# Projections, running sums and output projection as four column strips of 32 on TensorE

## The reference, cut to what matters

```python
# 8 batches, 512 tokens, 256 features, 16 heads of 16; everything f32
qkv = x @ w_qkv.T                      # q, k, v
L   = (q @ k^T) / 4                    # per head
L_y = (q @ (x @ w_ky.T)^T) / 4
agg = sum(exp(clip(L_y, -15, 15)) * mask) + 1e-6
w   = softplus(log(|L| + 1e-6) - log(agg + 1e-6)) * mask
A   = w / (sum(w) + 1e-6)
x   = layernorm(x + (A @ v) @ w_proj.T)
h   = silu(lin1(x)) * lin2(x)          # 256 -> 1024
h   = gelu(lin_h1(h)); h = gelu(lin_h2(h))
x   = layernorm(x + lin3(h))           # 1024 -> 256
```

## Time and profile before

| | |
|---|---|
| median of 3 runs | 1381.5 us (1379.47 to 1383.17) |
| profiled execution | 1381.93 us, its span 1380.1 us |
| PE busy | 1271.8 us (92%), 8310 matmul records |
| DVE busy | 720.5 us (52%) |
| ACT busy | 616.0 us (45%) |
| POOL busy | 118.2 us (9%) |
| mean granted TensorE clock | 0.985 |

### The profile page before, as it was taken

The page is one execution under the profiler, slowest core; times in us unless marked ns, Lnnn a source line. Parts: engine busy times, 40 slices in busy tenths (PEclk is TensorE's granted clock), DMA queues, the critical chain, the costliest instruction groups (busy, mean ns, idle before and its releaser), DMA issues.

```text
span 1380.1 us, 22940 instructions
## 1 busy us (share of the span) xinstructions
PE 1271.8 (92%) x8310; PEld 813.9 (59%) x8310; DVE 720.5 (52%) x1223; ACT 616.0 (45%) x810; POOL 118.2 (9%) x140
## 2 busy tenths in 40 slices
PE   5988999999999999985499999999999999999996
PEld 1433444444344444432388788787887878878785
DVE  2556767676777768576143533535235353343523
ACT  3566767667676766654132412323123241332411
POOL 1111111211112111110000000000000000000000
PEclk9999999999999999998699999999999999999998
DMA  2002222222221321000460000000000000000000
GB/s 74 16 17 69 94 62 92 76 91 76 79 102 47 106 76 54 1 32 16 170 251 16 31 0 15 30 15 30 0 15 30 15 30 0 15 30 15 30 0 16
DMA packets 31944, 66.89 MB, mean 48 GB/s; under 512 B 2849, under 2 KB 8609, under 8 KB 31905
## 3 DMA queue, kind: packets, MB, share of 16 engines
q1 hardware_dynamic: 31904, 66.35, 14.2%
HBM read 46.42 MB, written 19.92 MB: 48 GB/s over the span
## 4 chain that ended last, share of the span: by engine, by line
issue 51%; POOL 0%; DVE 0%; POOLq 0%; DVEq 0%
POOL f_rstd L813 0%; DVE f_res L820 0%; POOLq L913 0%; DVEq L825 0%; POOL f_minus_half L911 0%; POOLq L83 0%
## 5 line engine op out<-in xcount | busy, mean ns | idle before, releaser
L939 ACT ACTIVATE f_h_full<-f_layer_bank,f_scales 128x512 f32<-128x512 f32 x128 | 88.0, 687 | 354.7 <-PE f_layer_bank L1053 354.6
L502 DVE TENSOR_TENSOR w_ring<-score_banks,keep 128x1024 int32<-128x1024 int32 (+1 forms) x192 | 191.7, 1040 | 56.9 <-PE score_banks L651 56.9
L353 ACT ACTIVATE e_ring<-score_banks 128x1024 f32<-128x1024 f32 (+1 forms) x192 | 158.8, 879 | 136.9 <-PE score_banks L651 136.6
L1053 PE MATMUL f_layer_bank<-f_ha_hi,f_w_all 128*128 128x512 f32 x512 | 204.2, 399 | 2.7 <-DVE f_h_full L981 2.3
L1053 PE MATMUL f_layer_bank<-f_ha_lo,f_w_all 128*128 128x512 f32 x512 | 202.6, 396 | 0.0
L1053 PE MATMUL f_layer_bank<-f_hb_hi,f_w_all 128*128 128x512 f32 x512 | 202.5, 396 | 0.0
L1053 PE MATMUL f_layer_bank<-f_hb_lo,f_w_all 128*128 128x512 f32 x512 | 202.3, 395 | 0.0
L493 DVE TENSOR_SCALAR e_ring<-e_ring 128x2048 f32<-128x2048 f32 (+1 forms) x96 | 100.4, 1046 | 118.0 <-ACT e_ring L353 117.9
L360 ACT ACTIVATE w_ring<-w_ring 128x2048 f32<-128x2048 f32 (+1 forms) x96 | 156.7, 1632 | 7.2 <-DVE w_ring L502 7.0
L287 POOL TENSOR_SCALAR_AFFINE_SELECT e_ring<-e_ring 128x512 f32<-128x512 f32 (+1 forms) x96 | 78.5, 818 | 475.8 <-DVE e_ring L493 475.0
L651 PE MATMUL score_banks<-q,ky 32*128 32x512 f32 (+3 forms) x1024 | 98.1, 475 | 22.4 <-DVE w_ring L502 19.3
(11 more groups left out here) (101 smaller groups left out, 1534.7 us busy)
## 6 DMA issues: line engine op xcount, KB each, us to landing
piece<-in_wf SPq DMA_DIRECT2D x44, 256.0 KB, 2.8
wf_copy<-piece SPq DMA_DIRECT2D x44, 256.0 KB, 2.9
f_w_all<-wf_copy SPq DMA_DIRECT2D x2, 4096.0 KB, 24.8
f_x_turn<-x SPq DMA_DIRECT2D x9, 512.0 KB, 3.3
xq<-in_xt SPq DMA_DIRECT2D x8, 512.0 KB, 3.3
xv<-in_xt SPq DMA_DIRECT2D x8, 512.0 KB, 3.5
res<-in_xn SPq DMA_DIRECT2D x8, 512.0 KB, 4.1
x<-res SPq DMA_DIRECT2D x8, 512.0 KB, 2.8
```

Source lines behind the costliest of these rows:

```text
L353: nc.scalar.activation(e_ring[:, t % RING, 2 * i:2 * i + 2, 0:cols], pair_banks(y_pair(t, i), cols), ACT.Exp).then_inc(exp_done, 1)
L502: nc.vector.tensor_tensor(w_ring[:, t % RING, 2 * i:2 * i + 2, 0:cols].bitcast(I32), pair_banks(w_pair(t, i), cols).bitcast(I32), keep[:, ...
L939: nc.scalar.activation(h_full[m % 2][:], f_bank[m % RING][:], ACT.Gelu, scale=scales[:, 1 + layer, m:m + 1]).then_inc(gelu_done, 1)
L1053: mm = nc.tensor.matmul(out, left.bitcast(dt), right.bitcast(dt), start=first and n == 0, stop=last and n == 1)
```

## The change

A helper `in_strips` issues a matmul as four matmuls. Each has 32 of the 128 stationary columns, writes 32 of the 128 output partitions, and streams the same moving operand. It takes the place of the single matmul in `project_t`, `v_proj`, `sum_values` and `project_out`. Transposes, scores and sums stay as they are. No wait and no semaphore changes: the increment still sits on the last matmul of a step.

```diff
+            def in_strips(out, left, right, start, stop):
+                for r in range(QUAD):
+                    mm = nc.tensor.matmul(out[lanes(r)], left[:, lanes(r)], right, start=start, stop=stop)
+                return mm
             def project_t(u, kind, x, done):
...
-                    mm = nc.tensor.matmul(misc[:], w_in[:, kt, kind, m], x[:, kt, :], start=kt == 0, stop=kt == DT - 1)
+                    mm = in_strips(misc, w_in[:, kt, kind, m], x[:, kt, :], kt == 0, kt == DT - 1)
...  v_proj
-                        mm = nc.tensor.matmul(misc[:, tok], xv[:, kt, tok], w_in[:, kt, 3, m], start=kt == 0, stop=kt == DT - 1)
+                        mm = in_strips(misc[:, tok], xv[:, kt, tok], w_in[:, kt, 3, m], kt == 0, kt == DT - 1)
...  sum_values
-                mm = nc.tensor.matmul(misc[:], tri[:, 0, :], values.rearrange("p i h d -> p (i h) d"), start=True, stop=False)
+                mm = in_strips(misc, tri[:, 0, :], values.rearrange("p i h d -> p (i h) d"), True, False)
                 for i in range(1, TI):
                     for j in range(i):
-                        mm = nc.tensor.matmul(misc[:, P * i:P * i + P], tri[:, 1, :], v_aug[v.half][:, j, :, 0:HD],
-                                              start=False, stop=(i == TI - 1 and j == i - 1))
+                        mm = in_strips(misc[:, P * i:P * i + P], tri[:, 1, :], v_aug[v.half][:, j, :, 0:HD],
+                                       False, i == TI - 1 and j == i - 1)
...  project_out
-                        mm = nc.tensor.matmul(misc[:, D * i2:D * i2 + D], att_t[:, ct, tok], wp[:, ct, :],
-                                              start=ct == 0, stop=ct == DT - 1)
+                        mm = in_strips(misc[:, D * i2:D * i2 + D], att_t[:, ct, tok], wp[:, ct, :], ct == 0, ct == DT - 1)
```

## The result

| | before | changed |
|---|---|---|
| median | 1381.99 us (1379.47 to 1383.17) | 1392.06 us (1391.26 to 1393.94) |
| ratio | | 1.0076, 95% interval 1.006 to 1.0092 |
| profiled execution | 1381.93 us, span 1380.1 | 1392.66 us, span 1390.9 |
| PE busy | 1271.8 us | 1264.2 us |
| matmul records | 8310 | 10710 |

The prediction, 1367.5 us within 1362 to 1383, was wrong by 24.6 us and on the wrong side. TensorE's busy time fell by 7.6 us and the span grew by 10.8.

A forecast was written before the change was run, and what follows sets the result against it. TensorE's pace was taken to bound the attention phase. Savings of 9.4 us in five turns, 2.3 before the loop and 2.2 after, say 14, took 1381.9 to 1367.9, median 1367.5; range 1362 to 1383.

The forecast's parts named there:

- The cost of a change of form, and of each step: Whole-array steps pay 0.11 us at start, 0.10 at end; column strips save 0.19 to 0.22 us on each changed step.
- What of it reaches the end: Per loop turn, 1.88 us of 76.8 reaches the end; q_proj saves zero, v_proj counts in full in one slot of two.
- Issue of narrow strips: Rival, chance 0.08: instruction issue bounds the narrow strips, costing 4.0 us a unit, 64 in all, giving 1432.
- The near bound: At scores after an idle stretch, starts under 10 ns each: four pairs issue in 0.07 us, against 0.11 needed.
- the rival's case: Issue at 0.06 us a pair: v_proj's 64 pairs take 3.9 us for 1.76; chance 0.08.
- The skill's price for issue: Skill page: starts at least about 25 ns apart, about 62 ns a matmul without hardware decode, so v_proj alone 4.0 us.
- Four reads of one operand: Rival, chance 0.05: strips reading the same moving operand hold each other up; streaming 12% slower eats all that is won.
- The loop's code: Rival, chance 0.15: grown loop code is no longer kept; four branches back cost 10 to 13 us, giving 1377.5 to 1380.5.
- 2.3 had been taken for them: Four slots before the loop: 2.8 us saved in full, taken as 2.3 because they start with loads and an empty pipeline.

The follow-up runs named there:

- the one with two turns and no strips: Kernel before the change, whole-array steps, with two turns in TensorE's loop body and the fifth turn as straight code: 1389.35 us, ratio 1.0054.
- The whole-array control: Kernel before the change, whole-array steps, with TensorE's slot loop written out as straight code: 1382.3 us, ratio 1.0007.

## Why the prediction was wrong, by its own steps

- *The cost of a change of form, and of each step.* Right, each within 0.02 us.
- *What of it reaches the end.* Right: 1.88 us a turn was the sum, 76.8 less 74.90 is 1.90. `q_proj` gave nothing, as worked out, and idle time ahead of `v_proj` grew (0.27 us where it had none; in the other slot of the turn 0.34 for 0.25), with its start still on `q_keep`.
- *Issue of narrow strips.* The near bound was right. All 64 pairs of `v_proj` kept to the streaming time, 1.74 us; in the rival's case it would have been 3.9.
- *The skill's price for issue.* The sentence of the Trainium skill (page "TensorE: Matmul & The Clock Gate", section "Wait — 56ns, not 53.3ns?") on 25 ns between starts, and 62 ns a matmul with hardware decode off, gives prices that are not seen here. 64 matmuls in 1.74 us are 27 ns each, far under 62. Within a set of strips four start in under 0.04 us, closer than 25 ns.
- *Four reads of one operand.* No cost: a 512-wide set starts 0.43 us ahead of the next (410.91 to 411.34), as whole-array records do, and the 16 sets of `v_proj` take 0.11 each, as the sums' strips do.
- *The loop's code.* This is the step that failed. The mechanism was among the rivals, with about the right size of the body (0.14 MB, 0.12 by the straight code's rate) and the right number of branches, but with a chance of 0.15 and two terms too small. The price of a branch was taken from the one at 1368.0, 3421 ns; it is 4.3 to 4.9 us, and of it 3.9 to 4.5 were idle time of TensorE. And a stall's second cost was left out: TensorE's clock, which stood at the half level behind each, and made the next steps 2.1 to 2.8 us longer. So four branches back cost 26.5 us and not 10 to 13, and the case comes to 1394.0 where 1377.5 to 1380.5 stood. Measured were 1392.1. With the right price it would have been the slower rival, and the range would have had to reach it.
- *What the chances missed.* The size of the code was in the rows: 600 records over 1292, and the sign that a body of 1400 was kept while a jump elsewhere was not. No row showed the limit, and an unknown limit with the body growing by half deserved a chance near that of the forecast.

With the loop written out the prediction's own time came: 1367.9 for 1367.5. That is partly luck in the size. Straight code has a cost that the working did not hold (below): its turns save 1.6 us each where the sum had 1.88. The slots before the loop gave some of that back: the first `turn` in the loop came 3.2 us earlier (150.83 for 154.05), where 2.3 had been taken for them.

## What to carry to other kernels

Count the instructions that a change adds inside a loop that an engine branches back over, against what a turn has now, before the time of the steps is worked out. If the trace shows no instruction DMAs in later turns and a short branch, the code is kept; a change that lets it outgrow that pays the fetch at every branch back, and on TensorE the half clock behind it as well. Where an engine's steps stand between work in column strips, doing them in column strips too saves about 0.2 us each, if the code still fits. Straight code is the way out where it does not, at 0.3 us a turn here.

## What was not expected of the hardware

- *The clock falls at a stall of 4 to 5 us.* There are 6.8 us at 0.50 around the end of the stall of each branch back, in the changed kernel and in the one with two turns and no strips, and 4.0 to 5.7 us of them are TensorE's work. That work took 2.0 to 2.8 us longer for it.
- *Waits in straight code are slower than in the loop.* This is a beat 3 to 4 in the strips kernel with the loop written out, VectorE's first absolute instruction and TensorE's scores that wait for it:

```profile
394.03 1.23 DVE L518 TENSOR_TENSOR w_ring<-score_banks,keep 128x1024 int32<-128x1024 int32 x1 [0.16 <-PE score_banks L673]
...
395.40 1.15 PE L673 MATMUL score_banks<-q,ky 32*128 32x128 f32 x16 [0.56 <-DVE w_ring L518]
```

and this the same place in the kernel before, whose scores started at 442.42:

```profile
441.14 1.22 DVE L502 TENSOR_TENSOR w_ring<-score_banks,keep 128x1024 int32<-128x1024 int32 x1 [0.36 <-PE score_banks L651]
```

From the end of the one to the start of the other it is 0.14 us in straight code (395.26 to 395.40) and 0.06 in the loop (442.36 to 442.42). Strips have no part in it, and nor has writing out a loop: in the slots ahead of the loop, which are straight code in every kernel, the kernel before has 0.14 us too, from the end of this instruction (98.37) to the scores at 98.51:

```profile
97.14 1.23 DVE L502 TENSOR_TENSOR w_ring<-score_banks,keep 128x1024 int32<-128x1024 int32 x1 [0.37 <-PE score_banks L651]
```

The written-out turn is 75.19 us, not 74.90, most likely for this:

```profile
376.67 0.66 PE L757 MATMUL misc_bank<-ident,base_v 128*128 128x128 f32 x4
...
451.86 0.66 PE L757 MATMUL misc_bank<-ident,base_v 128*128 128x128 f32 x4
```

The whole-array control has the same 0.28 us a turn (77.09 for 76.81), but its time does not show it (1382.3 for 1382.1). Whether it is the wait on a constant instead of a register, or something else of straight code, was not tried.
- *The limit is sharp,* between 1712 and 1760 records a turn, and what sets it (size alone, or where pieces of 16 KB fall) stays open.
